# Expert stream in steps of two expert pairs, GpSimd taken out of it, attention of the next chunk dealt among the steps

## The reference, cut to what matters

```python
h = _layernorm(x) * (1 + ca) + sa
x = x + ga * attn(h)          # rmsnorm; linear to gate and val (256 each); two depthwise convolutions of val
                              # (4 taps, then A and Bm; 9 taps, then silu, pw); ha, hb, fuse; gate; out
h = _layernorm(x) * (1 + cb) + sb
probs = jax.nn.sigmoid(x @ router_w.T + expert_bias)
top_w, top_idx = jax.lax.top_k(probs, 8)              # normalised, times 2.5, scattered into combine (T, 160)
h1 = jax.nn.silu(jnp.einsum('th,eih->eti', x, w_gate))   # 160 experts, 64 hidden values each
h1w = h1 * combine.T[:, :, None]
routed = jnp.einsum('eti,ehi->th', h1w, w_down)
shared = jax.nn.silu(x @ w_gate_shared.T) @ w_down_shared.T
x = x + gb * (routed + shared)
```

## Time and profile before

| | |
|---|---|
| median of 3 runs | 716.9 us (716.49 to 720.12) |
| profiled execution, first to last instruction | 715.5 us; no other time of it was recorded |
| busy DVE / PE / POOL / ACT | 629.3 / 557.4 / 543.0 / 457.4 us |
| granted PE clock, mean | 0.918 of full |
| HBM | 97.54 MB read, 2.36 MB written, 140 GB/s |

### The profile page before, as it was taken

The page is one execution under the profiler, slowest core; times in us unless marked ns, Lnnn a source line. Parts: engine busy times, 40 slices in busy tenths (PEclk is TensorE's granted clock), DMA queues, the critical chain, the costliest instruction groups (busy, mean ns, idle before and its releaser), DMA issues.

```text
span 715.5 us, 9691 instructions
## 1 busy us (share of the span) xinstructions
PE 557.4 (78%) x2354; PEld 239.4 (33%) x2354; DVE 629.3 (88%) x726; ACT 457.4 (64%) x814; POOL 543.0 (76%) x382
## 2 busy tenths in 40 slices
PE   4851676976769795987688796896697799999994
PEld 3521322422324342432234342432243343333331
DVE  5899888999895967999897866999899779999995
ACT  4682855875547655875556775695456777677773
POOL 3267077867896777867797686867699689999996
PEclk9995589999898899999898899899898999999999
DMA  7224573433434163433334274433334255445440
GB/s 251 88 89 147 165 249 122 150 123 109 145 118 147 62 250 120 146 118 114 121 125 139 77 232 125 143 117 117 117 117 146 89 194 185 158 172 172 158 167 15
DMA packets 31739, 100.19 MB, mean 140 GB/s; under 512 B 3360, under 2 KB 7776, under 8 KB 31584
## 3 DMA queue, kind: packets, MB, share of 16 engines
q1 hardware_dynamic: 29360, 97.81, 40.5%
q10 hardware_dynamic: 2352, 2.10, 0.9%
HBM read 97.54 MB, written 2.36 MB: 140 GB/s over the span
## 4 chain that ended last, share of the span: by engine, by line
POOL 57%; issue 29%; DVE 8%; DMA 2%; PE 1%; POOLq 1%; ACT 1%; SPq 1%; ACTq 0%; DVEq 0%
POOL gw_l L354 53%; DVE cv L634 2%; DMA gw<-wg_dram 1%; POOL xt L343 1%; DVE mod L536 1%; DVE wg_l L619 1%; DMA cbr<-combine 1%; POOL s_l L332 1%; POOL mat L335 1%; POOL mat L340 1%; POOLq L353 0%; DVE s_l L696 0%; DVE mat L727 0%; DVE z_l L643 0%; POOL rstd L349 0%
## 5 line engine op out<-in xcount | busy, mean ns | idle before, releaser
L354 POOL TENSOR_TENSOR gw_l<-gw,gw_h 128x512 f16<-128x512 f32 x320 | 471.4, 1500 | 130.6 <-ACT gw_h L488 129.9
L771 DVE TENSOR_TENSOR gw<-gw,cbr 128x512 f32<-128x512 f32 x320 | 386.8, 1253 | 54.0 <-ACT gw L504 30.4
L488 ACT ACTIVATE gw_h<-gw 128x512 f16<-128x512 f32 x320 | 200.8, 628 | 165.7 <-DVE gw L771 165.1
L504 ACT ACTIVATE gw<-bank 128x512 f32<-128x512 f32 x320 | 187.6, 587 | 33.8 <-PE bank L809 30.0
L807 PE MATMUL bank<-h_h,wg_h 128*128 (+1 forms) x320 | 128.3, 401 | 35.7 <-ACT gw L504 35.7
L807 PE MATMUL bank<-gw_h,wd_h 128*128 128x512 f16 x320 | 126.5, 395 | 23.1 <-POOL gw_l L354 16.2
L808 PE MATMUL bank<-h_h,wg_l 128*128 (+1 forms) x320 | 126.4, 395 | 0.0
L809 PE MATMUL bank<-h_l,wg_h 128*128 (+1 forms) x320 | 126.1, 394 | 0.0
L808 PE MATMUL bank<-gw_h,wd_l 128*128 128x512 f16 x320 | 124.9, 390 | 0.0
L809 PE MATMUL bank<-gw_l,wd_h 128*128 128x512 f16 x320 | 124.7, 390 | 0.0
L634 DVE SCALAR_TENSOR_TENSOR cv<-vp,vec,cv 128x512 f32<-128x512 f32 x64 | 71.6, 1118 | 1.3
(11 more groups left out here) (197 smaller groups left out, 544.0 us busy)
## 6 DMA issues: line engine op xcount, KB each, us to landing
cbr<-combine SPq DMA_DIRECT2D x160, 512.0 KB, 4.1
gw<-wg_dram SPq DMA_DIRECT2D x10, 512.0 KB, 4.7
gw<-wd_dram SPq DMA_DIRECT2D x10, 512.0 KB, 3.7
mat<-mats_dram SPq DMA_DIRECT2D x1, 1392.0 KB, 7.7
combine<-mat ACTq DMA_DIRECT2D x4, 256.0 KB, 2.1
out_dram<-ot SPq DMA_DIRECT2D x4, 256.0 KB, 4.2
xt<-x_dram ACTq DMA_DIRECT2D x3, 256.0 KB, 4.5
...
```

The source lines that it names most:

```text
L354: g.tensor_tensor(gw_l[:, k, :], gw[:, k, :], gw_h[:, k, :], ALU.subtract).then_inc(s["lo_done"], 1)
L488: a(gw_h[:, k, :], gw[:, k, :], ACT.Copy).then_inc(s["hi_done"], 1)
L504: a(gw[:, k, :], up_ps[k % URING][:], ACT.Silu, scale=1.0 / ES_SCALE).then_inc(s["silu_done"], 1)
L771: e.tensor_tensor(gw[:, k, :], gw[:, k, :], cbr[:, k // 2, k % 2 * L:(k % 2 + 1) * L], ALU.mult)\
```

## The change

The kernel is rewritten as straight code, with no loop in it; `walk` writes the order out, once for all engines, and every engine fills in its own part of each name.

**The stream.** A step is a duo, two pairs of experts (four experts), 40 duos a chunk, 160 in all. Its silus go from two PSUM banks (U0, U1) into the halves of one slot of `sr` (128x1024 f32, four slots); DVE multiplies the slot in place with one `combine` load of 128x1024 (L901), ACT copies it to f16 (`gh`, L621) and DVE, not POOL, subtracts (`gl`, L897). The down products stand three duos behind (LAG). One DMA a duo, three duos ahead.

```diff
-            def low(c, i8, k):
...
-                g.tensor_tensor(gw_l[:, k, :], gw[:, k, :], gw_h[:, k, :], ALU.subtract).then_inc(s["lo_done"], 1)
...
-            def high(c, i8, k):
...
-                a(gw_h[:, k, :], gw[:, k, :], ACT.Copy).then_inc(s["hi_done"], 1)
...
-            def weigh(c, i8, k):
...
-                e.tensor_tensor(gw[:, k, :], gw[:, k, :], cbr[:, k // 2, k % 2 * L:(k % 2 + 1) * L], ALU.mult)\
-                    .then_inc(s["gw_done"], 1)
...
@@ ACT
+            def duo(J):
+                def silu(q):
+                    act.wait_ge(s["up_ps"], 2 * J + q + 1)
+                    a(sr[J % SRING][:, q * L:(q + 1) * L], U[q][:], ACT.Silu, scale=1.0 / ES).then_inc(s["s_done"], 1)
+                if J < ALL:
+                    if J >= SRING:
+                        act.wait_ge(s["lo_set"], J - SRING + 1)
+                    elif J == 0:
+                        act.wait_ge(s["wb_ps"], 1)
+                        act.wait_ge(s["win_lo"], 1)
+                    silu(0)
+                if J >= DUOS and J % DUOS == LAG:
+                    evict(J // DUOS - 1)
+                if 1 <= J <= ALL:
+                    n = J - 1
+                    act.wait_ge(s["gm"], n + 1)
+                    if n >= GRING:
+                        act.wait_ge(s["dn_ps"], n - GRING + 1)
+                    elif n == 0:
+                        act.wait_ge(s["mod_ps"], 2 * B)
+                        act.wait_ge(s["rr_set"], 2)
+                    a(gh[n % GRING], sr[n % SRING], ACT.Copy).then_inc(s["hi_set"], 1)
+                if J < ALL:
+                    silu(1)
@@ DVE
+            def duo(J):
+                if 1 <= J <= ALL:
+                    n = J - 1
+                    dve.wait_ge(s["hi_set"], n + 1)
+                    e.tensor_tensor(gl[n % GRING], sr[n % SRING], gh[n % GRING], ALU.subtract).then_inc(s["lo_set"], 1)
+                if J < ALL:
+                    dve.wait_ge(s["s_done"], 2 * J + 2)
+                    dve.wait_ge(ld_c[J % CRING], 16 * (J // CRING + 1))
+                    e.tensor_tensor(sr[J % SRING], sr[J % SRING], cr[J % CRING], ALU.mult).then_inc(s["gm"], 1)
@@ PE, duo(J), with n = J - LAG
+                for q in range(2):
+                    if J < ALL:
+                        if J < DUOS and q == 0 and J % (PER // 2) == 0:
+                            pe.wait_ge(s["w_lo"], 2 * (J // (PER // 2)) + 1)
+                        if J:
+                            pe.wait_ge(s["s_done"], 2 * J + q - 1)
+                        b = J // DUOS % 2
+                        split(U[q][:], pair(J, q, 0), (x_h[b][:], x_l[b][:])).then_inc(s["up_ps"], 1)
...
+                        mm(Y[:], sdw[:], ss32[:], start=True, stop=False).then_inc(s["sd_ps"], 1)
...
+                        w_ = slice(q * L, (q + 1) * L)
+                        last = split(Y[:], pair(n, q, 1), (gh[n % GRING][:, w_], gl[n % GRING][:, w_]), start=False,
+                                     stop=(d == DUOS - 1 and q == 1))
+                        if q:
+                            last.then_inc(s["dn_ps"], 1)
```

```diff
+FIRST = {
+    0: ("ya0", "silu1"), 1: ("ya1",), 2: ("gate",), 3: ("tanh", "yb0"), 4: ("yb1", "gy0"), 5: ("gy1", "wo"),
+    6: ("orow",), 7: ("orow_lo",), 9: ("o0",), 10: ("o1", "base0"), 11: ("base1",), 12: ("x2",), 13: ("bn",),
+    14: ("rstd2",), 15: ("t2",), 16: ("h2m",), 17: ("h2a",), 19: ("turn2",), 20: ("table", "h2T"), 21: ("xl", "logit"),
+    22: ("prob", "shup"), 23: ("ss", "max"), 24: ("swap", "cw"), 25: ("sum",), 27: ("cT",), 28: ("cT_sb",), 29: ("c_out",),
+}
+LATER = {
+    0: ("turn",), 1: ("hnT",), 2: ("conv0a",), 3: ("conv0b",), 4: ("conv0c",), 5: ("conv1a", "silu0"), 6: ("conv1b",),
+    7: ("conv1c",), 8: ("gate", "silu1"), 9: ("ya0", "tanh"), 10: ("ya1", "wo"), 11: ("yb0", "orow"), 12: ("yb1", "gy0", "orow_lo"),
+    13: ("gy1", "base0"), 14: ("base1",), 15: ("o0",), 16: ("o1",), 17: ("x2",), 18: ("bn",), 19: ("rstd2",), 20: ("t2",),
+    21: ("h2m",), 22: ("h2a",), 24: ("turn2",), 25: ("table", "h2T"), 26: ("xl", "logit"), 27: ("prob", "shup"), 28: ("ss", "max"),
+    29: ("swap", "cw"), 30: ("sum",), 32: ("cT",), 33: ("cT_sb",), 34: ("c_out",),
+}
+NORM = {31: ("t1",), 32: ("hm",), 33: ("ha",), 34: ("square",), 35: ("rms",), 36: ("hi",), 37: ("low",)}
...
+    for c in range(B):
+        plan = {0: FIRST, B - 1: {}}.get(c, LATER)
+        for d in range(DUOS):
+            duo(c * DUOS + d)
+            if d == LAG and c:
+                end(c - 1)
+            for n in plan.get(d, ()):
+                att(c + 1, n)
+            if c + 2 < B:
+                for n in NORM.get(d, ()):
+                    att(c + 2, n)
+            if c == 0 and d % 2 == 1 and ready < PIECES:
+                piece(ready, ready + 1)
+                ready += 1
+            if c == 0 and d in (26, 30):
+                setup(10 + (d == 30))
+    for d in range(LAG):
+        duo(ALL + d)
+    end(B - 1)
```

```diff
+            def taps(q, k0, i0, i1, w_h, w_l, bk, start, ready):
+                for i in range(i0, i1):
+                    if ready and i % (KS // SYMQ) == 0:
+                        pe.wait_ge(s["wc_lo"], i // (KS // SYMQ) + 1)
+                    w = slice(i * DI + q * P, i * DI + (q + 1) * P)
+                    split(bk[:], (w_h[:, w], w_l[:, w]),
+                          (hnT[:, 0, i + k0:i + k0 + L], hnT[:, 1, i + k0:i + k0 + L]),
+                          start=start and i == i0, stop=False)
...
+                elif n[0:4] == "conv":
+                    q, i = int(n[4]), "abc".index(n[5])
+                    bk = (A1, A2)[q]
+                    if i == 0:
+                        pe.wait_ge(s["hnT_set"], c + 1)
+                        if c:
+                            pe.wait_ge(s["gy_set"], 2 * (c - 1) + q + 1)
+                    taps(q, 0, 3 * i, 3 * i + 3, wc_h, wc_l, bk, i == 0, c + q == 0)
+                    if i == 2:
+                        if c + q == 0:
+                            pe.wait_ge(s["sc_lo"], 1)
+                        mm(bk[:], rsym[:, q * P:(q + 1) * P], k("isym", 64), start=False, stop=True).then_inc(s["conv_ps"], 1)
```

More of the change, by code:

```diff
@@ new lines, with walk @@
+NORM = {31: ("t1",), 32: ("hm",), 33: ("ha",), 34: ("square",), 35: ("rms",), 36: ("hi",), 37: ("low",)}
+def walk(setup, att, piece, duo, end):
+    setup(0)
+    att(0, "stat")
+    att(0, "nb")
+    setup(1)
+    att(0, "t1")
+    att(0, "hm")
+    att(0, "ha")
+    setup(2)
+    att(0, "square")
+    setup(3)
+    att(0, "rms")
+    setup(4)
+    att(0, "hi")
+    att(0, "low")
+    att(0, "turn")
+    att(0, "hnT")
+    setup(5)
+    att(0, "conv0a")
+    att(0, "conv0b")
+    setup(6)
+    att(0, "conv0c")
+    att(0, "silu0")
+    att(0, "wo")
+    att(0, "base0")
+    att(0, "base1")
+    att(1, "stat")
+    att(0, "conv1a")
+    att(0, "conv1b")
+    att(0, "conv1c")
+    setup(7)
+    att(0, "silu1")
+    att(0, "gate")
+    att(0, "tanh")
+    setup(12)
+    att(0, "orow")
+    att(0, "orow_lo")
+    att(1, "nb")
+    piece(0, 3)
+    att(1, "t1")
+    att(1, "hm")
+    att(1, "ha")
+    att(0, "ya0")
+    att(0, "ya1")
+    setup(8)
+    att(1, "square")
+    att(1, "rms")
+    att(0, "yb0")
+    att(0, "yb1")
+    att(0, "gy0")
+    att(0, "gy1")
+    att(1, "hi")
+    att(1, "low")
+    att(0, "o0")
+    att(0, "o1")
+    setup(9)
+    piece(3, 5)
+    att(1, "turn")
+    att(0, "x2")
+    att(1, "hnT")
+    att(0, "bn")
+    att(0, "rstd2")
+    att(1, "conv0a")
+    att(1, "conv0b")
+    att(0, "t2")
+    att(0, "h2m")
+    att(0, "h2a")
+    att(1, "conv0c")
+    att(0, "turn2")
+    att(0, "table")
+    att(0, "h2T")
+    att(0, "xl")
+    att(0, "logit")
+    att(0, "prob")
+    att(0, "shup")
+    att(0, "ss")
+    att(1, "conv1a")
+    att(0, "max")
+    att(0, "swap")
+    att(0, "cw")
+    att(0, "sum")
+    att(1, "silu0")
+    att(1, "conv1b")
+    att(0, "cT")
+    att(0, "cT_sb")
+    att(0, "c_out")
+    piece(5, 6)
+    att(1, "conv1c")
+    ready = 6
+    for c in range(B):
[17 more added lines that the diff above has]
+    end(B - 1)
@@ L244, in build, with pair, HB, nothing @@
+        def pair(J, q, kind):
+            u = (J % DUOS) * 2 + q
+            i, at = 2 * (u // PER) + kind, u % PER * P
+            return high(i, at, P), low(i, at, P)
+        def HB(c):
+            return h if c else h0
+        def nothing(*_):
+            return None
         block = ctx.enter_context(nc.Block())
@@ L299, in _, with end @@
+            def end(c):
+                sp.wait_ge(s["fin"], c + 1)
+                sp.dma_start(ov[c], res[:, c * NT:(c + 1) * NT]).then_inc(s["out_st"], 16)
+            walk(nothing, att, nothing, duo, end)
+            sp.wait_ge(s["out_st"], 16 * B)
         @block.gpsimd
@@ L985, in finish @@
-            def finish(c):
-                for k in range(BODY - LAG, BODY):
-                    last = down(c, BODIES - 1, k)
-                last.then_inc(s["acc_ready"], 1)
-                pe.wait_ge(s["acc_sb"], c + 1)
```

(18 more changed lines are left out.)

1425 lines of the change are left out of this document (737 added, 688 removed).

## The result

The changed kernel takes 714.22 us (median of 11 runs, 711.81 to 717.22) against 716.49 us before (11 runs, 715.23 to 720.12). The ratio is 0.9964, 95% interval 0.9946 to 0.9982: 0.36% faster, where 1.1% was forecast. The time lies inside the range, 5.2 us from the forecast, but the gain is 2.3 us where 8 were expected. So two questions stay: whether the account by terms was right, and why a change that takes all of the stream from POOL and 72 operations from DVE moves so little.

What follows compares the result with a forecast made beforehand. No engine was full; POOL and DVE slowed each other, and the change would be bound by a ring of copy, subtraction and multiply. 88.1 + 551.7 + 58 + 9.9 = 707.7 us of span, 709 us of time; range 686 to 735.

Steps and rivals of the forecast that it cites:

- The ring: In the stream, ACT's copy, DVE's subtraction and the next multiply run in series: 3.47 us a duo, 551.7 us for 159.
- The overflows: Attention work dealt into the stream's gaps that does not fit: 17 + 2 x 20.1 + 1 = 58 us over four passes.
- PE's and ACT's share: Passes 1 and 2: PE's convolution, gate and boundary work 14 us net a pass, ACT's sigmoids with table loads 4.9 us.
- DVE's 1.2 us: Passes 1 and 2: replacing the maxima and the weights in one step, and three small ones, 1.2 us a pass.
- the 7.0 us of attention in the odd steps of pass 0: Weight pieces fill both gaps in odd steps, so eight of them pay their attention on DVE in full, 7.0 us.
- The start: Time until the first multiply: 88 us, against 92.56 before; called the softest term, 80 to 100.
- Time less span: Measured median less the profiled execution's span, 1.4 us, added to the forecast span of 707.7 us.
- Rival 3: PE falls to its lower clock at table loads and boundaries, 2.8 us each; nine give 25 us, 734 us; chance 0.20.
- Rivals 2 and 4: 2: dearer ring handoffs, 719 or 728 us, chance 0.16; 4: gaps take nearly all attention, 685 us, chance 0.12.
- rival 5: Each table load costs its length twice: 12 x 1.28 = 15.4 us in the ring, 724 us; chance 0.03.
- rival 6: The ring isn't closed and PE sets the pace, below 660 us; chance the remaining 0.02.
- the end: Time from the start of the last multiply to the kernel's end: 9.9 us, against 11.5 before.

Runs made afterwards that it cites:

- part 3: Two edits to the changed kernel: only the first of three matmuls per convolution tap in chunks 2 and 3, 701.35 us; router's sigmoid computed by tanh, 701.82 us.
- Part 4: Two edits to the changed kernel's start: POOL's 18 operations for the first folding put first, 711.86 us; weight pieces 3 and 4 converted later, 710.1 us.
- e1_both_orders: Changed kernel with both silus ahead of the previous duo's copy on ACT, and the multiply ahead of the previous duo's subtraction on DVE: 633.38 us.
- f8_pool_order: Changed kernel with the 18 small POOL operations that PE's first folding needs put first and released, the other 8 behind: 711.86 us.
- f5_conv_high: Changed kernel with only the first of three matmuls per tap in the convolutions of chunks 2 and 3, output less exact: 701.35 us.
- tanh run: Changed kernel with the router's sigmoid computed as tanh(z/2) + 1, so four table loads a chunk go: 701.82 us.

## Why the prediction was right or wrong

- **The ring** was right: its members, its order and its price (3.47 forecast, 3.483 measured), with DVE 68%, ACT 58% and PE 79% busy in the last pass for 68, 64 and 75. The two orders turned apart and together show that it is the bound. 0.013 us too little, 159 times, is 2.1 us.
- **The overflows** were right as a sum, 57.3 for 58, with some luck: pass 0 was 2.2 us cheaper, and pass 2 1.6 dearer because PE's clock fell at its boundary, a term that the sum doesn't have. PE's and ACT's share are shown by the runs of part 3; DVE's 1.2 us and the 7.0 us of attention in the odd steps of pass 0 were not tried.
- **The start** is the largest miss and the step that failed, in its size: 90.6 for 88.1. The folds were to be done at 19 us and are at 22.4: POOL's 26 small operations, which the forecast named but gave no row for, run from 7.1 to 15.9 us, 0.34 us each, and PE waits 5.3 us for the last. Part 4 shows that 2.1 to 3.0 us of that wait go with their order. Luck has a part in the 2.5 us: in six executions of kernels with the same start the first multiply stands at 87.9 to 90.2. PE takes 8.6 us from its first folding to the first convolution in the changed kernel and 7.1 to 7.2 in four of the six, whose clock is at its upper level in a part of that stretch.
- **Time less span** was taken as 1.4 us and is 2.5 here. The 1.4 was the median of some executions of before less the span of another one. Within one execution before takes 1.8 to 2.2 us more than its span (27 executions) and the changed kernel 2.5 (11), so about half of the miss is the mixing and half is the kernel's.
- **Rival 3**, PE at its lower level in the stream, did not decide the time, but its mechanism came once: at the boundary of pass 2, for 1.7 us where the rival had 2.8 a time. None of the table loads of this execution did it. In the executions of e1_both_orders, f8_pool_order and f5_conv_high it came at two, two and three boundaries. **Rivals 2 and 4** fall with the ring's 3.483 and with the overflows; **rival 5** falls with the tanh run; **rival 6** with the first row of the ring.

So 2.5 for the start, 2.1 for the ring, 1.1 for time less span, less 0.7 for the overflows and with 0.1 for the end: 5.1 of the 5.2 us. The forecast gain, 8 us, was the difference of two sums over 700. The miss of 5.2 us is 0.7% of either sum and two thirds of that gain; the start's range alone, 80 to 100, was wider than the gain.

Where the expected gain went: DVE and POOL no longer slow each other and PE has the convolution, yet copy, subtraction and multiply follow each other in one circle at 3.48 us a duo where before took 3.13. PE, the engine with the most work, idles 0.9 us in each. The better order on two engines takes 81 us off the changed kernel.
